# Summing the second layer's residual rows in PSUM and copying them on ScalarE

## What is computed

```python
x = x + tanh(g_xattn[0]) * L0_xattn(layernorm(x), ctx)
x = x + tanh(g_ffn[0])   * L0_ffn(layernorm(x))          # 8 experts, one chosen per row
x = x + tanh(g_xattn[1]) * L1_xattn(layernorm(x), ctx, ctx)
x = x + tanh(g_ffn[1])   * L1_ffn(layernorm(x))          # ternary weights, rounded activations
```

```python
q = query @ Wq + bq;  k = key @ Wk + bk;  v = value @ Wv + bv
attn = softmax(q k^T * 16**-0.5)
return (attn v) @ Wo + bo
```

## Time and profile before

| | |
|---|---|
| median of three runs | 620.09 us |
| the profiled execution's own time | 621.87 us |
| its span in the profile | 620.1 us |
| busy: TensorE matmul (PE) | 503.2 us, 81% |
| busy: VectorE (DVE) | 378.4 us, 61% |
| busy: ScalarE (ACT) | 259.0 us, 42% |
| busy: GpSimd (POOL) | 252.0 us, 41% |
| L1503, residual rows of both layers | 32 instructions, of which 16 in layer 1 |

### The profile page before, as it was taken

How to read it: one execution, slowest core, us unless ns; L and a number is a source line. 1 busy time by engine, 2 the same in 40 slices (tenths; PEclk the granted TensorE clock), 3 DMA queues, 4 the chain that set the end, 5 groups by cost and what they waited for, 6 DMA issues and landing times.

```text
span 620.1 us, 10588 instructions
## 1 busy us (share of the span) xinstructions
PE 503.2 (81%) x3550; PEld 394.2 (64%) x3558; DVE 378.4 (61%) x718; ACT 259.0 (42%) x441; POOL 252.0 (41%) x322
## 2 busy tenths in 40 slices
PE   5956978889794499999999999939487787568994
PEld 2533856658583289999999999934345455334653
DVE  4277889798824735253334422215788998868993
ACT  1233846355370054343334332311354454526884
POOL 3363434253410162021111011037255868737996
PEclk9966999999596589999999999985789999688999
DMA  6930010100146224842574201013000000000101
GB/s 207 297 120 1 1 34 1 35 1 0 35 162 210 72 87 170 295 163 65 189 237 159 95 17 34 8 51 93 10 1 1 2 0 1 1 1 0 35 34 68
DMA packets 28630, 46.37 MB, mean 75 GB/s; under 512 B 2380, under 2 KB 24920, under 8 KB 26552
## 3 DMA queue, kind: packets, MB, share of 16 engines
q1 hardware_dynamic: 24328, 39.02, 18.7%
q0 software_dynamic: 1680, 4.59, 2.5%
q10 hardware_dynamic: 2592, 2.36, 1.1%
HBM read 38.36 MB, written 7.60 MB: 74 GB/s over the span
## 4 chain that ended last, share of the span: by engine, by line
PE 46%; DVE 29%; issue 8%; POOL 7%; ACT 5%; DMA 3%; DVEq 0%; ACTq 0%; SPq 0%; POOLq 0%
PE s_tile L919 20%; PE bank L931 7%; DVE p_sum L1374 5%; DVE s_max L1360 5%; PE bank L780 3%; DVE probs L1365 3%; PE bank L664 3%; DVE stats L1298 3%; PE s_tile L997 2%; DVE ew L1320 2%; DVE xn L1320 2%; POOL probs L472 2%; ACT probs L1064 2%; DVE x_res L1503 1%; PE bank L765 1%
## 5 line engine op out<-in xcount | busy, mean ns | idle before, releaser
L919 PE MATMUL s_tile<-q_t,ew 128*128 128x128 f32 x1152 | 137.0, 278 | 1.5 <-DVE probs_t L1632 0.9
L919 PEld LDWEIGHTS s_tile<-q_t,ew 128*128 128x128 f32 x1152 | 133.1, 194 | 3.2 <-DVE probs_t L1632 2.2
L472 POOL TENSOR_TENSOR probs<-probs,p_rcp 128x1024 f32<-128x1024 f32 x32 | 60.9, 1906 | 111.2 <-DVE p_rcp L1377 111.2
L1632 DVE TENSOR_TENSOR probs_t<-s_tile,probs 128x512 f32<-128x512 f32 x36 | 24.9, 690 | 78.8 <-ACT probs L1186 78.8
L693 PE MATMUL bank<-ident,probs 128*128 128x128 f32 x256 | 39.7, 305 | 30.3 <-POOL probs L472 28.8
L693 PEld LDWEIGHTS bank<-ident,probs 128*128 128x128 f32 x256 | 32.4, 156 | 42.0 <-POOL probs L472 31.0
L531 POOL TENSOR_TENSOR token_now<-token_of,carried 128x1 uint32<-128x1 uint32 x17 | 4.6, 272 | 127.5 <-PE bank L905 127.5
L1064 ACT ACTIVATE probs<-probs 128x1024 f32<-128x1024 f32 x32 | 33.9, 1058 | 51.4 <-DVE probs L1365 51.4
L1094 ACT COPY probs_t<-bank 128x512 f32<-128x512 f32 x64 | 34.8, 589 | 43.9 <-PE bank L693 43.8
L1360 DVE TENSOR_REDUCE s_max<-s_tile 128x16 f32<-128x1024 f32 x32 | 38.4, 1199 | 18.0 <-PE s_tile L677 17.9
L1186 ACT ACTIVATE probs<-s_tile 128x512 f32<-128x512 f32 x36 | 21.6, 599 | 63.3 <-PE s_tile L919 63.3
(11 more groups left out here) (212 smaller groups left out, 1102.6 us busy)
## 6 DMA issues: line engine op xcount, KB each, us to landing
ew<-in_L_ffn_w SPq DMA_DIRECT2D x8, 2048.0 KB, 7.8
ew<-in_L_ffn_w SPq DMA_DIRECT2D x8, 1024.0 KB, 5.9
slots_y<-xn ACTq DMA_DIRECT2D x18, 128.0 KB, 1.9
x_res<-in_x SPq DMA_DIRECT2D x4, 512.0 KB, 6.7
token_rows<-ew SPq DMA_DIRECT2D x4, 512.0 KB, 3.2
out_rows<-x_res SPq DMA_DIRECT2D x3, 512.0 KB, 2.9
w<-in_L_xattn_W SPq DMA_DIRECT2D x2, 512.0 KB, 9.0
ew<-in_L_ffn_w_gate SPq DMA_DIRECT2D x1, 1024.0 KB, 8.6
```

The source lines that it names most:

```text
L472: nc.gpsimd.tensor_tensor(p, p, p_rcp[:, i, :].unsqueeze(2).to_broadcast([P, H, M]), ALU.mult).then_inc(s["p_norm"], 1)
L919: last = nc.tensor.matmul(o[:, P * j:P * j + P], ew1[:, s, k, c0:c0 + P], xs_t[:, par, k, :], start=(k == 0), stop=(k == DK - 1))
```

## The change

The residual rows of layer 1 are built in PSUM. For each row tile TensorE first multiplies the identity matrix by the tile's rows of `x_res` into the bank, and then adds the two products with `wo` to it. ScalarE copies the sum to `x_res`, four copies for each batch, in place of VectorE's L1503. The gate moves into the copy of the attention's values to `o_t`, which becomes an activation with a scale. TensorE takes over the wait for the bias (`p_xb`). ScalarE copies rows 0 and 1 ahead of `exps(b + 1, 1)` and rows 2 and 3 behind it. VectorE does `sums(b + 1, 1)` directly behind `scores(b + 1, 1)`, and then waits for all four rows ahead of `norm_stats`. Layer 0 stays as it is.

```diff
@@ TensorE, attention, l == 1
-                    pe.wait_ge(s["a_o"], 2 * DK * b + 2 * DK)
+                    pe.wait_ge(s["p_xb"], b + 1)
                     for i in range(TB):
                         if i == 1 and not first_batch:
                             pe.wait_ge(f["a_x"], b)
+                        nc.tensor.matmul(new_bank[i][:, 0:D], ident[:],
+                                         x_res[:, bass.ds(TB * b + i, 1), :].rearrange("p o d -> p (o d)"),
+                                         start=True, stop=False)
+                        if i == 0:
+                            pe.wait_ge(s["a_o"], 2 * DK * b + 2 * DK)
                         for k in range(DK):
-                            last = nc.tensor.matmul(att_bank[1][i][:, 0:D], o_t[:, k, P * i:P * i + P], wo[:, k, :],
-                                                    start=(k == 0), stop=(k == DK - 1))
+                            last = nc.tensor.matmul(new_bank[i][:, 0:D], o_t[:, k, P * i:P * i + P], wo[:, k, :],
+                                                    start=False, stop=(k == DK - 1))
                         last.then_inc(s["t_y"], 1)
@@ ScalarE, attention
                 def output(half, k):
                     act.wait_ge(s["t_o"], 2 * DK * b + DK * half + k + 1)
-                    nc.scalar.copy((o_hi if l == 0 else o_t)[:, k, 2 * P * half:2 * P * half + 2 * P],
-                                   x_bank[k][:, 0:2 * P]).then_inc(s["a_o"], 1)
+                    cols = slice(2 * P * half, 2 * P * half + 2 * P)
+                    if l == 0:
+                        nc.scalar.copy(o_hi[:, k, cols], x_bank[k][:, 0:2 * P]).then_inc(s["a_o"], 1)
+                    else:
+                        nc.scalar.activation(o_t[:, k, cols], x_bank[k][:, 0:2 * P], ACT.Identity,
+                                             scale=tg[:, 1:2]).then_inc(s["a_o"], 1)
+
+                def new_row(i):
+                    act.wait_ge(s["t_y"], TB * b + i + 1)
+                    nc.scalar.copy(x_res[:, bass.ds(TB * b + i, 1), :].rearrange("p o d -> p (o d)"),
+                                   new_bank[i][:, 0:D]).then_inc(s["v_y"], 1)
...
+                if l == 1:
+                    new_row(0)
+                    new_row(1)
                 if not last_batch:
                     exps(l, b + 1, 1)
+                if l == 1:
+                    new_row(2)
+                    new_row(3)
@@ VectorE, attention
-                dve.wait_ge(s["p_xb"], b + 1)
+                if l == 0:
+                    dve.wait_ge(s["p_xb"], b + 1)
+                elif not last_batch:
+                    sums(l, b + 1, 1)
                 for i in range(TB):
-                    if l == 1 and i == 2 and not last_batch:
-                        sums(l, b + 1, 1)
                     g = TB * b + i
-                    dve.wait_ge(s["t_y"], g + 1)
-                    nc.vector.scalar_tensor_tensor(row(g), att_bank[l][i][:, 0:D], tg[:, l:l + 1], row(g), ALU.mult,
-                                                   ALU.add).then_inc(s["v_y"], 1)
+                    if l == 0:
+                        dve.wait_ge(s["t_y"], g + 1)
+                        nc.vector.scalar_tensor_tensor(row(g), h_bank[i][:, 0:D], tg[:, 0:1], row(g), ALU.mult,
+                                                       ALU.add).then_inc(s["v_y"], 1)
                     if last_batch:
                         dve.wait_ge(s["v_y"], g + 1)
                         row_stats(second, TB * b, (i,))
```

More of the change, by code:

```diff
@@ L70, in flamingo @@
         h_bank = [*t_bank, *x_bank]
-        att_bank = [h_bank, [*reversed(t_bank), *x_bank]]
+        new_bank = [*reversed(t_bank), *x_bank]
         ident = sb("ident", [P, P])
```

## The result

The changed kernel takes 625.38 us, the median of 11 runs (623.28 to 628.99), against 620.93 us for the kernel before, also the median of 11 (619.13 to 623.05). The ratio is 1.0073, with a 95% interval of 1.0056 to 1.0090: 4.5 us slower, between 3.5 and 5.6. The profiled execution took 625.38 us, with a span of 622.9.

A forecast was written before the change was run, and what follows sets the result against it. It saw two chains reach L1320 within 0.2 us: VectorE's own, and exponential, sums, GpSimd. The terms 0.45 + 1.06 + 0.44 + 1.75 = 3.7 us, on the median 620.09, gave 623.8 us, range 620.8 to 626.4.

The forecast's parts named there:

- the loop: Ends of batches 0, 1 and 2 together: later by 0.45, 1.06 and 0.44 us.
- Price of an identity product: TensorE, each row tile: two records at L802's 0.225 us from record to record, 0.45 us in all.
- The activation with a scale: ScalarE's copy to `o_t`: the scale adds below 0.1 us each, with nothing as the lower end.
- The 0.1 us a row for the address: ScalarE's loop register: row address priced at nothing where ScalarE waits, 0.1 us a row as upper end.
- End of batch 1, +1.06: Exponential starts behind row 1's copy, 1.06 us late; GpSimd's chain carries that to L1320.
- End of batch 0, +0.45: First identity product is free; exponential waits for row 1, 0.45 us late by the same GpSimd chain.
- End of batch 2, +0.44: GpSimd's lateness has time to vanish; only VectorE's own path counts, 0.44 us late.
- The tail, +1.75: End of the last batch: eight more records in series, with last copy and hand-over, move L997 by 1.75 us.
- eight records more, at the full clock: Last batch's identity products on TensorE: 8 x 0.225 = 1.8 us.
- The third rival: Tail stays longer at 1.2 GHz and loop hand-overs are dearer: 5.7 us slower, 625.8 us; chance 0.17.
- The faster rival: VectorE is the bound and its rows at ends of batches 0 to 2 are gone: -3.4 us, 616.7 us; chance 0.06.
- 0.2 us of air: GpSimd's chain ahead of L1320: `rstd` ends at 503.61, L1320 starts at 503.84, leaving up to 0.2 us slack.

The follow-up runs named there:

- e1: Changed kernel, with ScalarE taking the exponential of the next batch's tile 1 ahead of all four row copies; 623.27 us, ratio 1.0027 to the kernel before.
- e5: Changed kernel with the identity product kept, but VectorE copies the sums out of PSUM in the earlier order; 624.47 us, ratio 1.0077 to the kernel before.
- e6: Changed kernel with the exponential ahead of the four row copies and no identity product (residual and bias left out); 620.64 us, ratio 0.9994 to the kernel before.
- e3: Changed kernel, from batch 1 on with identity products of row tiles 0, 2 and 3 ahead of `ff_turn`; 626.97 us, ratio 1.0088 to the kernel before.
- e7: e6 with GpSimd making the feed-forward's rstd, in its own buffer, ahead of scaling rows; 621.32 us, ratio 0.9997 to the kernel before.
- e8: Kernel before; batches 0 to 2: identity product and ScalarE copy for tiles 2 and 3, rstd first; last batch: `ff_turn` behind the products; 619.20 us, ratio 0.9973.
- e10: e8 plus fourteen products that compute nothing, keeping TensorE at work in the last batch; 615.02 us, ratio 0.9905 to the kernel before.
- e11: Changed kernel plus fourteen products that compute nothing, keeping TensorE at work in the last batch; 623.87 us, ratio 1.0050 to the kernel before.
- e12: Kernel before, with `ff_turn` behind the last batch's products and fourteen products that compute nothing; 615.80 us, ratio 0.9907 to the kernel before.

## Why the prediction was right

It forecast 623.8 us against a median of 620.09, 3.7 us more; measured are 4.5 us, in an interval of 3.5 to 5.6, and 625.38 us lie in the range of 620.8 to 626.4. The verdict (slower by more than 0.5%) held, with the line at 3.1 us. The mechanism held in the loop and at the tail. That the sum comes so near is in part luck: the loop was forecast at 1.95 us and lost 1.60, the tail at 1.75 and lost 2.44, and the two errors go against each other.

**Price of an identity product.** 0.45 us was taken from L802. A tile of six records takes 1.30 to 1.40 us (495.52 - 494.12 and on), 0.22 to 0.23 a record. Held. The activation with a scale takes 0.47 us where the copy took 0.37: 0.1, the upper end of what was read from L1059 and L1094. The 0.1 us a row for the address came from no row of the trace. Nothing of it is seen: row 2's copy starts at 497.10, when the exponential (496.08 + 1.06) ends.

**End of batch 1, +1.06.** Measured 0.94, and by the mechanism given: VectorE idle 2.03 us, the exponential behind row 1, L1340 released by `rstd` after 0.61 us, 26.72 us from one to the next where 26.8 was forecast. e1 gives 0.66 of it to ScalarE's order.

**End of batch 0, +0.45.** Measured 0.36; e1 takes it away whole.

**End of batch 2, +0.44.** Measured 0.30, and unchanged in e1 and e5, so it is the last row. The same row has VectorE's statistics 0.29 us late at the end of batch 1, forecast as 0.44.

**The tail, +1.75.** This term was mis-sized: 2.44 in the profile. The step that was off is "eight records more, at the full clock"; the sentence's own terms make 1.79 us, not 1.75. It took the moment of the clock's rise in one profile for a property of the kernel. In the changed kernel's own profile the rise came later, in e1's earlier. With the full clock throughout it is 1.4 us, so about 1 us of the 2.44 is the clock. The third rival had this mechanism, with a chance of 0.17; its dearer hand-overs in the loop did not come. The measured 4.5 us lie between the forecast and it.

**The faster rival** was VectorE as the only bound. e6 refutes it from the other side: even with its work gone and nothing late, b stays at 25.78, on GpSimd's chain. The forecast's 0.2 us of air in that chain was wrong, as e6 showed. **The hidden case** said that the exponential slips by 0.2 us and no more; it slipped by 0.91, from 1.26 us behind the subtraction's start (495.94 - 494.68) to 2.17 (496.08 - 493.91).

**Still open.** The five stretches differ by 4.0 us, the medians by 4.5; one profile each can't say whether the half is chance. Part of it lies outside the span of the profile: over its eleven runs the changed kernel's time is 2.0 us longer than the span in the median (up to 3.1), the kernel before has 1.8. How often the tail falls on which moment of the clock wasn't counted.

## What to carry to other kernels

Work taken from the busiest engine gains only if it was on the path: rows that fill a wait for another engine cost nothing, and a copy put into an in-order queue costs the instruction behind it the wait for its producer. Before such a move, follow each chain into the next meeting point and compare their arrivals, and test an idle window for its own waits in the middle, as e3 had to learn. Where a serial product follows a few microseconds of waiting on TensorE, look at the granted clock first: fourteen products that compute nothing gained more here than any change to VectorE's work.

## What the runs showed of the chip that I had not expected

The same instructions of the last batch took 6.60 and 5.20 us in two profiles, because the clock rose at different moments. In e6 the clock fell to 0.50 for about 6 us inside the loop, after a stretch in which TensorE was half idle, and the products that followed came late. Six of the thirteen profiles have such a fall in the loop (e3, e6, e7, e8, e10, e11), and in e11 the stretch b, in which it lies, takes 26.72 us as in the changed kernel.

In e11 the clock stayed at 1.00 although TensorE had waited 3.4 us for GpSimd ahead of its last `ff_turn`; it had been at work nearly all the time before that wait. The Trainium skill (TensorE: Matmul & The Clock Gate, section What's actually happening) has the clock follow how busy the engine has been recently; e11 and e12 agree, with 1.00 in place of 0.50.
